# Roll layer of an early-fusion kernel: earlier bias additions, and another order of work in the step without an incoming group

## The reference

```python
z = einsum('bse,he->bsh', x, W_A) * SCALING      # x = layernorm(h), 16 heads
zp = transpose(softmax(z, axis=1), (0, 2, 1))
roll = zp[:, :, (i - j) % S] * tril              # causal, Toeplitz in i - j
v = einsum('bse,fe->bsf', x, W_V).reshape(B, S, H, D)
out = einsum('bhij,bjhd->bihd', roll, v)
h = h + einsum('bse,fe->bsf', out, W_O) + b_O
```

## Time and profile before

| | |
|---|---|
| time, median of 3 runs | 1249.98 us (1248.33 to 1250.88) |
| time of the profiled execution | 1249.16 us |
| span in its trace | 1247.4 us |
| PE busy | 1070.6 us, 86% |
| DVE busy | 653.4 us, 52% |
| POOL busy | 578.7 us, 46% |
| ACT busy | 438.0 us, 35% |
| mean granted TensorE clock | 0.916 of full speed |

### The profile page before, as it was taken

How to read it: one execution, slowest core, us unless ns; L and a number is a source line. 1 busy time by engine, 2 the same in 40 slices (tenths; PEclk the granted TensorE clock), 3 DMA queues, 4 the chain that set the end, 5 groups by cost and what they waited for, 6 DMA issues and landing times. The chain is left out here.

```text
span 1247.4 us, 25938 instructions
## 1 busy us (share of the span) xinstructions
PE 1070.6 (86%) x7433; PEld 887.3 (71%) x7448; DVE 653.4 (52%) x1585; ACT 438.0 (35%) x1149; POOL 578.7 (46%) x754
## 2 busy tenths in 40 slices
PE   8699999997864999999999987758888866988996
PEld 6477777776753999888888886335555545988995
DVE  2487777774699774333333336648887524101111
ACT  2255555552434444434333321313223212332331
POOL 0173333320132988767666637777860001333342
PEclk9799999997988999999999989778878857999999
DMA  6100000000102677677787743334360101455242
GB/s 217 37 1 1 0 0 0 0 1 18 56 1 89 216 207 222 185 226 195 216 233 208 229 123 102 101 102 127 110 219 18 34 26 35 136 199 190 72 133 89
DMA packets 78990, 136.39 MB, mean 109 GB/s; under 512 B 17180, under 2 KB 55839, under 8 KB 76480
## 3 DMA queue, kind: packets, MB, share of 16 engines
q0 software_dynamic: 19584, 52.59, 16.2%
q1 hardware_dynamic: 29952, 55.89, 13.6%
q10 hardware_dynamic: 29376, 27.01, 6.3%
HBM read 195.34 MB, written 36.04 MB: 185 GB/s over the span
## 5 line engine op out<-in xcount | busy, mean ns | idle before, releaser
L1224 POOL DMA_INDIRECT x_x<-m_x_rows,x_idx x200 | 196.9, 985 | 82.7 <-issue 39.9
L1247 PE MATMUL x_pup<-x_xt,x_w 128*128 128x128 f32 x1600 | 215.0, 278 | 15.8 <-DMA x_w<-in_experts 11.9
L1247 PEld LDWEIGHTS x_pup<-x_xt,x_w 128*128 128x128 f32 x1600 | 196.1, 193 | 21.0 <-ACT x_xt L1278 11.0
L1490 POOL DMA_INDIRECT rl_y<-m_y_rows,rl_idx x136 | 136.2, 1001 | 40.2 <-issue 39.8
L1318 DVE TENSOR_TENSOR x_hid<-x_gate,x_pup 128x128 f32<-128x128 f32 x200 | 57.5, 288 | 182.3 <-PE x_pdown L1256 148.2
L427 POOL TENSOR_TENSOR wa_kheads<-wa_kT,cst 128x544 f32<-128x544 f32 x64 | 73.0, 1149 | 133.3 <-PE wa_scores L506 87.6
L1256 PE MATMUL x_pdown<-x_w,x_hid 128*128 128x256 f32 x400 | 120.0, 382 | 0.3 <-DVE x_hid L1318 0.3
L1278 ACT ACTIVATE x_xt<-x_pturn 128x256 f32<-128x256 f32 x200 | 76.6, 383 | 99.9 <-PE x_pturn L1237 97.3
L2123 PE MATMUL x_pup<-x_xt,late_w 128*128 128x128 f32 x768 | 94.8, 284 | 12.2 <-DMA late_b<-in_b 9.4
L2123 PEld LDWEIGHTS x_pup<-x_xt,late_w 128*128 128x128 f32 x768 | 93.3, 200 | 16.2 <-issue 15.4
L2182 ACT ACTIVATE x_hid<-x_pup,late_b 128x128 f32<-128x128 f32 x192 | 54.6, 368 | 121.2 <-PE x_pup L2123 121.2
(11 more groups left out here) (286 smaller groups left out, 1918.4 us busy)
## 6 DMA issues: line engine op xcount, KB each, us to landing
x_w<-in_experts SPq DMA_DIRECT2D x200, 384.0 KB
late_w<-in_w SPq DMA_DIRECT2D x52, 1024.0 KB, 11.2
m_y_rows<-x_y ACTq DMA_DIRECT2D x200, 128.0 KB
m_x_rows<-xn SPq DMA_DIRECT2D x34, 128.0 KB, 1.8
x_x<-m_x_rows,x_idx POOLq DMA_INDIRECT x200
late_b<-in_b SPq DMA_DIRECT2D x24, 128.0 KB
patches<-in_patches SPq DMA_DIRECT2D x3, 864.0 KB, 11.8
rl_y<-m_y_rows,rl_idx POOLq DMA_INDIRECT x136, 2.7
```

The source lines that it names most:

```text
L1224: nc.gpsimd.indirect_dma_start(x[:, s, :], None, x_rows, bass.IndirectOffsetOnAxis(ap=idx[:, s:s + 1], axis=0))\
L1247: mm = nc.tensor.matmul(pup[:, s % 2, m * P:(m + 1) * P], w[:, s, (m * DC + c) * I0:(m * DC + c + 1) * I0], xt[:, s, c * P:(c + 1) * P], s ...
L1490: nc.gpsimd.indirect_dma_start(y[:, t % YR, kk, :], None, y_rows, bass.IndirectOffsetOnAxis(ap=idx[:, n:n + 1], axis=0))\
```

## The change

Two things change. POOL's loop adds the bias of a tile three tiles of gathers sooner (BEHIND is 4). And step 9, the only one with a middle group but no incoming one, gets its own order on PE, ACT and DVE: both halves of group 7 are multiplied, inverted and projected first, and tiles 12 and 13 are measured, normalised, turned and chosen behind that. Fill matmuls are put between: 8, 4 and 2 ahead of the projection, and 8 at the step's end.

```diff
--- before.py
+++ after.py
@@ -1481,7 +1481,7 @@
                     pool.wait_ge(normed, turn_at["in", t] + 1)
                     nc.gpsimd.tensor_tensor(h[:, t, :], h[:, t, :], late["b_o"][:, :], ALU.add).then_inc(biased, 1)
 
-                BEHIND = 7
+                BEHIND = 4
                 for t in range(NT):
                     if t >= YR:
                         pool.wait_ge(added, (t - YR + 1) * K0)
@@ -1635,6 +1635,21 @@
                         values(g1, 0)
                     if has2:
                         forward(g2, 1, 1)
+                    if has2 and not has1:
+                        fill(g2 + 1, 8)
+                        invert(g2, 0)
+                        fill(g2 + 1, 4)
+                        invert(g2, 1)
+                        fill(g2 + 1, 2)
+                        for m, ts in pairs_out(g2):
+                            project(g2, m, ts)
+                        for t in outs:
+                            turn("out", t)
+                            fill(g2 + 1, 1)
+                        for t in outs:
+                            choose(t)
+                        fill(g2 + 1, 8)
+                        continue
                     for t in outs:
                         turn("out", t)
                         fill_mid(g1, 1)
@@ -1730,6 +1745,14 @@
                     g1, g2, g3 = i - 1, i - 2, i - 3
                     has1, has2 = 0 <= g1 < NG, 0 <= g2 < NG
                     ins, outs = tiles_in(g1), tiles_out(g3)
+                    if has2 and not has1:
+                        move_out(g2, 0)
+                        move_out(g2, 1)
+                        root("out", outs)
+                        normalise("out", outs)
+                        for t in outs:
+                            move_turned("out", t)
+                        continue
                     if ins:
                         root("in", ins)
                         normalise("in", ins)
@@ -1851,6 +1874,14 @@
                         scale("in", tiles_in(g1))
                     for m, ts in pairs_out(g3):
                         add_projected(m, ts)
+                    if has2 and not has1:
+                        multiply(g2, 0)
+                        multiply(g2, 1)
+                        for t in outs:
+                            dve.wait_ge(proj_added, t // 2 + 1)
+                            measure("out", t)
+                        scale("out", outs)
+                        continue
                     for t in outs:
                         dve.wait_ge(proj_added, t // 2 + 1)
                         measure("out", t)
```

## The result

The changed kernel takes 1230.15 us (median of 4 runs, 1229.11 to 1230.88) against 1249.15 (1248.30 to 1250.88): ratio 0.985, 95% interval 0.983 to 0.986. The forecast was 1226, range 1219 to 1238. The profiled execution took 1229.69 us with a span of 1227.9, 19.5 us less than before. The roll layer gave more than that, and the layer behind it gave some back.

A forecast was written before the change was run, and what follows sets the result against it. It took DVE's addition waiting for POOL's late bias (Place A), the block of biases (Place B) and step 9 with the tail (Place C) as bounds: 11.5 + 2.0 + 10 = 23.5 us off 1249.16, so 1226 us, range 1219 to 1238.

The forecast's parts named there:

- Place A: Step 3: the first projection addition, held by POOL's late bias of tile 1, starts 11.5 us sooner, bounds 10.5 to 12.
- The term for the projection: Step 3: PE's projection, 2.64 us long, ends at 823.49 + 0.61 = 824.1 and then releases the first addition.
- the gathers kept their cover: Tiles 7 and 8: gathers behind three more biases still land 2.1 us before DVE combines them.
- The rival that something unnamed held the step: Step 3's addition is held by something the trace does not name: Place A gives -1.8 us, time 1239; chance 0.03.
- Place B: POOL's four-bias block at 926.23: DVE's stall beside it goes, 2.0 us gained, bounds -1.7 to 2.9.
- none above 1.5: Sign for Place B: no DVE instruction of line L1825 takes more than 1.5 us.
- The extreme of the prediction: Roll layer: every bias meets a two-input DVE instruction, Place B gives -7.9 us, time 1235; chance 0.06.
- Place C: Step 9 and the tail to the logits: the new order gains 10 us, range 7 to 12.
- a step of about 13 us: Step 9: addition of tiles 14 and 15 about 13 us after that of 12 and 13, before 22.8.
- the half-clock sum: Tail at half clock: projection ends at most 1006.5, gain 2.7, loss 4; Place C -1.3, time 1237; chance 0.17.
- The expert layer behind begins after all engines have met, and moves as a block: Expert layer behind the roll layer: it shifts whole, so the 23.5 us sum comes off the total time.
- a rival for the loop and the tail only: TensorE's clock: half speed in the tail, 1237, chance 0.17; or slower in the steps too, 1253, chance 0.05.

The follow-up runs named there:

- e4: The changed kernel run once more, unedited: 1230.5 us against 1246.9 for the kernel before, ratio 0.988.
- e1: The kernel before with only the earlier biases (BEHIND 4 for 7), step 9 in its old order: 1235.6 us against 1246.9, ratio 0.990.
- e5: The changed kernel without the 22 fill matmuls of step 9: 1229.9 us against 1248.2 for the kernel before, ratio 0.985.
- e8: The changed kernel with both first expert-layer tiles turned, and copied by ACT, ahead of the first up projection: 1228.3 us against the kernel before's 1248.2, ratio 0.984.
- e3: The kernel before with biases one tile later (BEHIND 8 for 7): 1259.9 us against 1246.9, ratio 1.011.
- e2: The changed kernel with BEHIND back at 7, so only step 9's new order: 1241.6 us against 1246.9 for the kernel before, ratio 0.995.
- e6: The changed kernel without the eight fills at the end of step 9: 1231.3 us against 1248.2 for the kernel before, ratio 0.986.
- e7: The changed kernel with eight fills for four between step 9's two inversions: 1228.3 us against 1248.2 for the kernel before, ratio 0.984.
- e11: The changed kernel with the edits of e7, e8 and e10 together: ratio 0.994 to the kernel before, on a chip where that took 1352.7 us.
- e9: The changed kernel with an unused matmul behind each of the gate table's first 16: ratio 0.998 to the kernel before, on the 1352.7 us chip.
- e10: The changed kernel with 32 unused matmuls ahead of the expert layer's first turn: ratio 0.996 to the kernel before, on the 1352.7 us chip.
- e12: The changed kernel a third time, unedited: ratio 0.994 to the kernel before, on the chip where that took 1352.7 us.

## Why the prediction was right, and where it was off

*Place A* (11.5 us forecast). The addition moved 11.3 us; 1.0 of it is that the layer's first gather already started at 741.58 and not 742.55, so 10.3 from the change. By the same count it is 11.1 in e4, 9.1 in e1 and 9.2 to 10.3 in e5 to e8, so the bounds of 10.5 to 12 were mostly missed. The term for the projection was too small: it kept the 2.64 us of the earlier trace rows, and took 3.56, with the clock at half.

```profile
820.79 3.56 PE L1569 MATMUL rl_pr<-late_w_o,xT 128*128 128x256 f32 x8
```

The next releaser was the projection, as forecast, and the gathers kept their cover: tile 7 was combined at 830.08, forecast 829.8. e3 settles the mechanism. The rival that something unnamed held the step is out.

*Place B* (2.0 forecast). From the first addition to that of tiles 10 and 11 it was 127.7 us (835.64 to 963.38) and is 126.4 (824.38 to 950.78): 1.3 us. The 3.61 us of the earlier trace rows are gone, but three instructions of the same line (now L1848) take 1.56 to 1.60 us, each beside one bias, so "none above 1.5" was wrong. The gain is partly luck too: in e2, where the block of four biases stands as before, DVE's instruction beside it takes 1.21 us and POOL's block 4.32, so the 3.61 us were one outcome of that meeting, and the same stretch is 127.1 us without the earlier biases.

```profile
926.27 1.21 DVE L1848 TENSOR_TENSOR rl_prod<-rl_term 68x512 f32<-68x512 f32 x1
```

```profile
925.69 4.32 POOL L1482 TENSOR_TENSOR h<-h,late_b_o 128x256 f32<-128x256 f32 x4
```

DVE's rows of one of the three in the changed kernel, and of the addition that reads PSUM:

```profile
914.55 1.60 DVE L1848 TENSOR_TENSOR rl_prod<-rl_term 68x512 f32<-68x512 f32 x1
...
926.38 0.69 DVE L1827 TENSOR_TENSOR h<-h,rl_pr 128x512 f32<-128x512 f32 x1 [3.26 <-PE rl_pr L1569]
```

POOL's biases beside them:

```profile
914.86 0.73 POOL L1482 TENSOR_TENSOR h<-h,late_b_o 128x256 f32<-128x256 f32 x1
926.02 2.08 POOL L1482 TENSOR_TENSOR h<-h,late_b_o 128x256 f32<-128x256 f32 x3
```

The block of three fell beside the addition and stretched nothing. Each of the three stretched instructions began 0.3 us ahead of its bias by the profile and ended 0.56 us behind it. With the lock that the Trainium skill, page SBUF — State Buffer, section "SBUF: two separate sides", describes for two SBUF inputs these ends agree; the recorded starts alone do not tell which of the two engines waits. The extreme of the prediction did not occur.

*Place C* (10 forecast): 9.5. The sum was near, its parts were not. I expected a step of about 13 us and 11 behind it, by a clock that is full in the inversions and falls later; it was 16.0 and 9.7, since the clock fell in the second inversion and was full behind the projection. The last eight fills, which I had counted as a delay, are worth 1.8 us of the tail in e6's trace. In the half-clock sum the terms of the prediction end the projection at 1006.7 and not 1006.5, and 1008.97 less that is 2.3, not 2.7; the rival's time would be 1237.4 instead of 1237.

*Not foreseen in the roll layer*: 1.6 us in step 8, whose second inversion and projection saw less of the half clock (2.42 and 2.71 us, before 3.10 and 3.62). It is no work of the change. e2, whose biases and step 8 are those of the kernel before, has the same 21.24, as has e1, while e6 with the whole change but its last fills has 22.63.

*The step that failed* is "The expert layer behind begins after all engines have met, and moves as a block". It begins with PE's clock fallen through the routing, and when the clock comes back and falls again is not the same relative to the work. That cost 4.2 us: 1.0 + 10.3 + 1.3 + 1.6 + 9.5 = 23.7 at the logits, less 4.2, is the 19.5 of the span. I had treated the clock as a rival for the loop and the tail only. That the 23.7 meet the forecast sum of 23.5 is luck. The change itself made 21.1 of them, short by 1.2 at A, 0.7 at B and 0.5 at C, and 2.6 came from elsewhere: the 1.0 of the earlier first gather and the 1.6 of step 8.

*Open*: whether the change makes the expert layer's longer stretch more likely (a trace of the old order on the third chip, or more traces of both on one chip, would tell), and what in the stream ahead makes the clock fall behind the gate table in some executions (changed kernel, e4, e6, e7, e8, e11, and with the old tail e3) and not in others (before, e1, e2, e5, e9, e10, e12). Of the ten profiles with the new order and fills in step 9 six show it. The clock records of the traces give one hint. Where the expert layer's code is unedited and the fall comes (changed kernel, e3, e4, e6, e7), the clock had come back from half 24.1 to 25.9 us behind the logits; in six of the seven traces without the fall it came back at 22.4 to 23.7 us. But e2 has 24.7 and no fall. The idle gap ahead is not needed for it (e8); the gate table's 24 columns are only a suspicion.

## What to carry to other kernels

When a strictly ordered engine does small jobs between long ones, look for who waits for the first small job, and compare its end with when the other thing that the waiter needs is done: the difference is the most that can be gained, and here 10.3 of the forecast 11.5 us came. In a drain step without new input, put the work that feeds the end ahead of the work that only trails. After a change at one place, compare each later stage against the same mark in both traces; here a stage of identical code took 2% longer in one trace than in another, mostly because TensorE's clock met it in another state.

## What the runs showed of the hardware

A DVE instruction with both inputs in SBUF is stretched by a GpSimd addition beside it (0.68 us to 3.61 beside four additions of 2.75 in all), and the stretching can go to the other side: in e2 the same meeting took 1.21 us on DVE and 4.32 on GpSimd. One with an input in PSUM kept its 0.69 us beside three additions of 2.08. TensorE's granted clock fell from full to half while PE was busy without a gap for over 12 us (e8), and the identical kernel showed a fall in this stage in two executions (changed kernel, e4) and not in a third (e12). On one chip the kernel before took 1352.7 us where others gave 1246.9 to 1249.2.
